# A cast moved from DMA to VectorE, and a scale-and-shift from VectorE to ScalarE, between attention and feed-forward of an AdaLN block

## The reference

```python
sa, ca, ga, sb, cb, gb = mod...                 # from silu(c) @ wmod, per batch element
h = _layernorm(x) * (1 + ca) + sa
x = x + ga * attention(h, W_qkv)                # 16 heads of 64, 2048 tokens, D = 1024
h = _layernorm(x) * (1 + cb) + sb
x = x + gb * ffn(h, w_gate, w_up, w_down)       # INNER = 4096
# ffn: weights rounded to -1, 0, 1 times a scale; activations rounded to 8 bits with
# scale = 127 / max|row|, before gate/up and again before down
```

## Time and profile before

| | us |
|---|---|
| median of 3 runs | 3794.0 (3778.2 to 3801.6) |
| profiled execution, its own time | 3791.6 |
| its span, slowest core (5) | 3789.7 |
| spans of the eight cores | 3760.2 to 3789.7 |
| granted TensorE clock of the cores, mean (1 is full speed) | 0.695 to 0.704 |
| busy in the span: PE / DVE / ACT / POOL | 2770.7 / 1666.8 / 1073.7 / 247.9 |

### The profile page before, as it was taken

The page is one execution under the profiler, slowest core; times in us unless marked ns, Lnnn a source line. Parts: engine busy times, 40 slices in busy tenths (PEclk is TensorE's granted clock), DMA queues, the critical chain, the costliest instruction groups (busy, mean ns, idle before and its releaser), DMA issues.

```text
span 3789.7 us, 29982 instructions; the slowest of 8 cores (3760.2 to 3789.7 us)
## 1 busy us (share of the span) xinstructions
PE 2770.7 (73%) x8156; PEld 762.3 (20%) x8156; DVE 1666.8 (44%) x2462; ACT 1073.7 (28%) x1183; POOL 247.9 (7%) x453
## 2 busy tenths in 40 slices
PE   6527854999999999999999993120866866866866
PEld 1103320111111111111111111010322322322322
DVE  0275652434243443334342432478454454454464
ACT  0100025324233333333242331112332232232232
POOL 0000000111011110111110110000000000000000
PEclk9758765666766666666667666555977977977977
DMA  6439811112011111122121214312413413413413
GB/s 207 155 132 250 233 67 32 50 43 58 25 50 50 50 48 35 44 51 50 44 57 25 50 45 152 113 56 89 133 59 117 136 59 117 137 58 120 139 54 109
DMA packets 210310, 331.58 MB, mean 87 GB/s; under 512 B 136113, under 2 KB 136370, under 8 KB 195810
## 3 DMA queue, kind: packets, MB, share of 16 engines
q1 hardware_dynamic: 167122, 226.88, 18.7%
q0 software_dynamic: 43024, 102.79, 10.5%
HBM read 289.68 MB, written 42.01 MB: 88 GB/s over the span
## 4 chain that ended last, share of the span: by engine, by line
PE 52%; DVE 23%; DMA 11%; ACT 7%; issue 5%; DVEq 1%; SPq 0%; ACTq 0%; POOL 0%; POOLq 0%
PE sps L742 13%; PE sps L735 13%; PE avps L779 5%; PE dops L783 5%; PE dps L1390 3%; DVE gq L1322 2%; DVE vq L1349 2%; PE avps L775 2%; DVE gpb L1226 2%; DVE gup L1239 2%; PE bcps L801 2%; DVE mab L1252 2%; ACT sgb L1234 2%; PE qkpsB L469 2%; ACT sgb L1244 2%
## 5 line engine op out<-in xcount | busy, mean ns | idle before, releaser
L751 ACT ACTIVATE PT<-sps 128x1024 bf16<-128x1024 f32 x512 | 524.3, 1024 | 514.7 <-PE sps L742 514.6
L808 DVE RECIPROCAL bcsb<-bcps 128x512 bf16<-128x512 f32 x64 | 214.9, 3358 | 943.6 <-PE bcps L801 923.0
L742 PE MATMUL sps<-Qc,Kc 64*128 64x512 bf16 x1024 | 521.5, 611 | 0.0
L735 PE MATMUL sps<-c,onesb 1*128 1x512 bf16 x1024 | 512.3, 600 | 9.2 <-DMA c<-C8h 8.5
L1212 PE MATMUL gps<-hA,tg 128*128 128x512 bf16 x1024 | 250.5, 388 | 192.0 <-DMA tu<-ternu 126.8
L779 PE MATMUL avps<-PT,Vc 128*64 128x512 bf16 x512 | 236.8, 463 | 22.8 <-ACT PT L751 22.8
L1216 PE MATMUL ups<-hA,tu 128*128 128x512 bf16 x1024 | 247.7, 386 | 0.0
L1335 PE MATMUL dps<-gq,td 128*128 128x512 bf16 x256 | 129.4, 608 | 160.5 <-DVE gq L1322 160.5
L783 PE MATMUL dops<-PT,onecb 128*1 128x512 bf16 x512 | 218.5, 427 | 0.0
L1234 ACT ACTIVATE sgb<-gpb 128x512 f32<-128x512 f32 x128 | 80.6, 629 | 439.0 <-DVE gpb L1226 439.0
L1390 PE MATMUL dps<-gq,td 128*128 128x512 bf16 x768 | 177.9, 395 | 29.6 <-DMA td<-ternd 29.5
(11 more groups left out here) (171 smaller groups left out, 2643.1 us busy)
## 6 DMA issues: line engine op xcount, KB each, us to landing
tg<-terng SPq DMA_DIRECT2D x128, 256.0 KB, 2.8
tu<-ternu SPq DMA_DIRECT2D x128, 256.0 KB, 3.2
td<-ternd POOLq DMA_DIRECT2D x32, 1024.0 KB, 6.1
wmb<-wmod SPq DMA_DIRECT2D x8, 2048.0 KB, 8.9
xs<-xT SPq DMA_DIRECT2D x16, 1024.0 KB, 5.8
mb<-wgT SPq DMA_DIRECT2D x8, 2048.0 KB, 10.4
mb<-wuT SPq DMA_DIRECT2D x8, 2048.0 KB, 9.5
mb<-wdT SPq DMA_DIRECT2D x8, 2048.0 KB, 8.1
```

The source lines that it names most:

```text
L735: p.inc(TE.matmul(sps[sp][:, n2 * 512:(n2 + 1) * 512], onesb[0:1, :], cb[0:1, cs:cs + 512], start=True, stop=False), eT)
L742: p.inc(TE.matmul(sps[sp][:, n2 * 512:(n2 + 1) * 512], lhsT, Qc[bp:bp + 64, q0:q0 + 512], start=False, stop=True, tile_position=(bp, 0)), eT)
L751: p.inc(S.activation(PT[hb][:, kt * 1024:(kt + 1) * 1024], sps[sp], AF.Exp, scale=0.125), eS)
L808: p.inc(V.reciprocal(bcsb, bcps[:]), eV)
```

## The change

Three edits, all between attention and the feed-forward stage.

1. x2 stage: the casting DMA from POOL's queue is gone, and with it POOL's waits for x2 of the same tile and for the matmuls of tile d-2. DVE makes the bf16 copy with `tensor_copy` behind x2, and waits for the matmuls of tile d-2 ahead of it. PE waits for DVE in place of the DMA.
2. `emit_h2_pass`: the scale and shift are an Identity activation on ACT, with scale and bias columns, in place of DVE's `tensor_scalar`. It acts in both passes. DVE waits, ahead of the multiplication of tile d, for the activation of tile d-2, since that reads `x2b`.
3. The consumers: abs in pass A waits for ACT itself; in pass B DVE's `vq` waits for the activation of its tile.

```diff
-                p.wait(V, "V", "dcb%d" % buf, use_tok[(d - 2, "x2v")])
                 p.wait(V, "V", eS, use_tok[(d - 2, "x2s")])
...
-            dcb = "dcb%d" % buf
-            p.wait(G, "G", eV, tok_x2)
+            p.wait(V, "V", eV, tok_x2)
             if d >= 2:
-                p.wait(G, "G", eT, use_tok[(d - 2, "mm")])
-            use_tok[(d, "x2v")] = p.dma(G, "G", dcb, xbb[buf], x2b[buf])
-            if d >= 2:
+                p.wait(V, "V", eT, use_tok[(d - 2, "mm")])
                 p.wait(S, "S", eT, use_tok[(d - 2, "mm")])
+            p.wait(V, "V", eV)
+            p.inc(V.tensor_copy(xbb[buf], x2b[buf]), eV)
+            use_tok[(d, "x2v")] = p.cnt[eV]
...
-            p.wait(TE, "T", dcb, use_tok[(d, "x2v")])
+            p.wait(TE, "T", eV, use_tok[(d, "x2v")])
...
+                p.wait(V, "V", eS, h2tok[d - 2])
...
-            p.wait(V, "V", eV)
-            p.inc(V.tensor_scalar(h2sb[buf], x2b[buf], bvec[:, d:d + 1],
-                                  sbv[:, d:d + 1], ALU.mult, ALU.add), eV)
-            h2tok[d] = p.cnt[eV]
+            tok_x2n = p.cnt[eV]
+            p.wait(S, "S", eV, tok_x2n)
+            if d >= 2:
+                sm_, tk_ = hread(d - 2)
+                p.wait(S, "S", sm_, tk_)
+            p.wait(S, "S", eS)
+            p.inc(S.activation(h2sb[buf], x2b[buf], AF.Identity,
+                               scale=bvec[:, d:d + 1], bias=sbv[:, d:d + 1]), eS)
+            h2tok[d] = p.cnt[eS]
...
-        p.wait(S, "S", eV, h2tok[d])
+        p.wait(S, "S", eS, h2tok[d])
...
             p.wait(V, "V", eT, tok_sb)
+            p.wait(V, "V", eS, h2tok[d])
```

## The result

| | before | changed |
|---|---|---|
| median of 10 runs, us | 3787.6 (3778.2 to 3801.6) | 3721.8 (3711.9 to 3744.7) |
| ratio | | 0.9834, 95% interval 0.9810 to 0.9858 |
| the same pair once more, on another occasion | 3799.3 (9 runs) | 3724.3 (4 runs), ratio 0.9807 (0.9782 to 0.9832) |

Faster by 63 us by the first ratio (0.0166 x 3787.6) and by 73 by the second; the forecast was 3725 and 67.6 saved.

What follows compares the result with a forecast made beforehand. Bounds: in the x2 stage the load's place behind the cast in POOL's queue, in the passes DVE. 48.8 + 9.4 + 9.4 = 67.6 us saved from 3791.6 (median 3794.0) gave 3725, own range 3710 to 3738, with rivals 3703 to 3748.

Steps and rivals of the forecast that it cites:

- Part 1: x2 stage: cast moved to DVE frees the load from its place behind it; 48.8 us saved, ends 54 and 45.
- The steps: x2 stage, first x to last: 89.7 us before, 7 x 6.5 = 45.5 after; 44.2 us saved.
- the tail: x2 stage, last x to first matmul: 9.14 us before, 4.55 after without the casting DMA; 4.6 us saved.
- The period: x2 stage, time of one tile after the change: taken as 6.5 us, ends 5.7 and 7.1.
- the loop: x2 stage: landing, x, square, hand-overs and POOL's issue in turn, landing + 5.05 us for two tiles.
- a floor of 5.7: x2 stage: load 3.07 us plus store 2.65 us of all sixteen DMA engines; a tile can't go under 5.7 us.
- the landing: x2 stage, time for a load to land: 6.0 us alone, 9.2 with store and cast, about 8 taken.
- Part 2: Passes A and B: scale and shift go from DVE to ACT, Identity 2.1 us; 9.4 us saved in each.
- (a): Rival, x2 stage: DMA engines slower, 236 GB/s, 8.9 us a tile; 32 us saved instead of 49, total 3742; 20%.
- (b): Rival, passes: ACT becomes the chain and they give nothing; 49 us saved alone, total 3743; 6%.
- (c): Rival, x2 stage: load still held back another way; 27 us saved there, 46 with the passes, total 3746; 7%.
- (d): Rival, feed-forward stage: shorter pause leaves TensorE's clock at 0.66; 179 us lost, total 3903; 3%.

Runs made afterwards that it cites:

- reorder: Kernel before, with POOL issuing the load of tile d+1 ahead of the casting DMA of tile d; 3763.4 us, ratio 0.9923 to the kernel before.
- hold: Changed kernel, with POOL's load of tile d again waiting for x of tile d-1; 3764.4 us, ratio 0.9911 to the kernel before.
- p2_only: Changed kernel with the casting DMA put back on POOL's queue, scale and shift still on ACT; 3774.5 us, ratio 0.9945 to the kernel before.
- no_sq: Changed kernel without POOL's wait, ahead of a load, for the square of tile d-2; 3723.5 us.
- ident2: Changed kernel with each Identity activation done twice, same result; 3745.5 us, ratio 0.9885 to the kernel before.

## Why the prediction was right, point by point

**What bounds.** Right: in the x2 stage the load's place in POOL's queue, shown by the pair reorder and hold; in the passes DVE, shown by p2_only, where taking 1.35 us of each tile off DVE shortens each pass by 9 us.

**Part 1, 48.8 us.** Measured 48.9 in B. The steps: 7 tiles, forecast 44.2, measured 43.8 (88.4 - 44.6); the tail, forecast 4.6, measured 5.1 (B - A, 47.2 and 42.1). The period was taken as 6.5 between 5.5/5.7 and 7.1, and is 6.37 over the seven steps, 6.5 over the last five. But the reasoning behind it was only half right. I took the period from the loop, with the DMA engines as a floor of 5.7 under it. no_sq shows that the loop is not the bound; the transfers are, and they need more than I had taken: a load among stores takes 3.5 us of the engines as the mean of the cores, not the 3.07 of one load alone, and with the store that is 6.1 and not 5.7. The term was mis-sized by 0.4 us a tile, and the landing that I chose between the ends (about 8; measured 7.3 and 7.7) made up for it: that the loop's sum comes out at the period is so because a landing grows with the queue before it, and is luck as a forecast. That the shares of single windows can't be added up is seen in reorder too, there from the other side (8.7 against 7.54).

**Part 2, 9.4 and 9.4 us.** Measured 9.6 and 9.1. Identity 2.09 for the 2.1 taken; the periods 7.19 and 10.97 as worked out. No table load came with Identity. The estimate by the Trainium skill (ScalarE: Activation LUTs, "What ACT_TABLE_LOAD costs") was 2.08 and the trace agrees; the advice of the same page of the Trainium skill ("Rules for kernel authors") to leave multiply and add to VectorE holds for the single instruction (2.09 against 1.35 us) and was rightly not followed, as DVE was full and ACT was not.

**The rivals.** (a), DMA at 236 GB/s, is out: 325 GB/s in the middle of the stage. Its mechanism, the DMA engines as the bound, was nearer to the truth than my own loop; only its price was not. (b) is out: DVE waits for the Identity in tile 0 alone, and ident2 shows where waiting would begin. (c) is out, as each load is issued behind the square and not behind the next x; its price was too small: with the load held, a tile takes 11.1 us and not 9.6, since I had taken the landing of a load alone and it has a store beside it. (d) is out at its price: after the shorter pause cores 0 to 3 have a granted clock of 0.98 to 1.00 in all gate and up stretches (0.93 to 1.00 before), where 0.66 was feared. The 110 us of lighter work that the prediction names against it are in no row of it; in 2830 to 2940 of the kernel before TensorE was busy for 69.9 of 110 us at a granted clock of 0.70.

**The sum.** 67.6 forecast, 67.6 in the three stages of the profile, 63 and 73 by the two ratios of whole runs. That the first two agree to the digit is luck among terms that are each off by up to half a microsecond.

## What to carry to other kernels

Before an operation is moved because of its own cost, look at what stands behind it in its queue: here a load that needed nothing waited behind a cast, and swapping the two alone brought 36 of the 49 us, without moving the cast at all. Work moves well from a full engine to an idle one even where it takes longer there (2.09 us for 1.35), as long as something of the same length lies between its input and its reader; where nothing does, as in the first tile, the difference is paid. A wait for "everything so far" costs as much as the chain that it closes: exact waits for two loads per pass brought another 27 us in two passes.

## What the runs showed of the hardware that I had not expected

- The time that a transfer takes of the DMA engines depends on its company: a 1 MB load 2.7 to 3.3 us of all sixteen alone (3.07 on core 5) and 3.3 to 3.6 among stores. A casting DMA took about 2.9 a tile before (what is left of its queue's time after a load's 3.07), and cost 1.1 us more a tile when added to a full stage, in which the share rose to 1.02.
- With the DMA engines full (share 0.96), a load that was issued 2 us earlier did not land earlier (7.5 us from issue became 10.4), and the queue that issued it made no difference (6.32 against 6.4 us a tile).
- A DMA issue on POOL beside a DVE cast took 0.89 to 0.96 us in place of 0.53, in each case seen, and ended 0.11 to 0.13 us behind the cast.
